# Moving a down projection out of a TensorE-bound feed-forward stage and into the out-projection sums of a scan stage

## The reference, cut to what matters

```python
xn = _layernorm(x, axis=-1)
x = x + attn(xn, ...) + ffn(xn, ...)
...
def ffn(x, w_gate, w_up, w_down):          # H, I = 512, 1408
    gate = fp4_linear(x, w_gate)           # fp4_linear quantises both operands in blocks of 16
    y = fp4_linear(x, w_up)
    h = silu(gate) * y
    return fp4_linear(h, w_down)           # quantises h, 1408 -> 512: the down projection
...
def attn(x, W_in, conv_w, ...):            # a selective scan, D_INNER 1024, 16 states
    x_branch, z = split(x @ W_in)
    xc = silu(conv(x_branch) + conv_b)     # 4 taps
    B, C, dt = split(xc @ W_x)
    h = h * exp(dt * A) + dt * xc * B      # for every token, per channel and state
    y = (sum over states of h * C + xc * D) * silu(z)
    return y @ W_out                       # 1024 -> 512: the out-projection
```

## Time and profile before

| | |
|---|---|
| time, median of 3 runs | 5827.97 us (5827.87 to 5835.2) |
| profiled execution, its own time | 5827.07 us |
| its span | 5824.2 us |
| weight stage | 0 to 178 us |
| feed-forward stage | 178 to about 1820 us |
| scan stage | about 1820 to 5824 us |
| busy: PE, DVE, ACT, POOL | 4979.6, 5035.1, 2768.5, 3627.0 us |
| granted TensorE clock, mean | 0.964 of 2.4 GHz |

### The profile page before, as it was taken

How to read it: one execution, slowest core, us unless ns; L and a number is a source line. 1 busy time by engine, 2 the same in 40 slices (tenths; PEclk the granted TensorE clock), 3 DMA queues, 4 the chain that set the end, 5 groups by cost and what they waited for, 6 DMA issues and landing times.

```text
span 5824.2 us, 78018 instructions
## 1 busy us (share of the span) xinstructions
PE 4979.6 (85%) x21764; PEld 3145.6 (54%) x21764; DVE 5035.1 (86%) x6343; ACT 2768.5 (48%) x4579; POOL 3627.0 (62%) x2810
## 2 busy tenths in 40 slices
PE   1799999999998688888888888888888888888867
PEld 1688888888885344444444444444444444444444
DVE  7666766666662699999999999999999999999998
ACT  1111111111111665666666666666666665666653
POOL 4333333333331687878778788787877878878785
PEclk9999999999999899999999999999999999999968
DMA  2111111111112122222222222222122222222111
GB/s 74 33 42 41 43 40 43 41 41 43 40 42 80 63 77 71 73 73 67 74 71 76 71 65 79 68 76 72 66 74 71 75 71 66 75 71 75 61 56 49
DMA packets 211700, 362.55 MB, mean 62 GB/s; under 512 B 26208, under 2 KB 58976, under 8 KB 207216
## 3 DMA queue, kind: packets, MB, share of 16 engines
q1 hardware_dynamic: 211312, 358.17, 19.9%
HBM read 287.80 MB, written 70.29 MB: 61 GB/s over the span
## 4 chain that ended last, share of the span: by engine, by line
DVE 32%; issue 14%; PE 12%; ACT 5%; POOL 3%; DVEq 1%; DMA 0%; ACTq 0%; SPq 0%; POOLq 0%
DVE hs L1095 20%; DVE acc L1109 11%; PE ht L1212 4%; PE mm L1201 4%; POOL v L919 3%; ACT decay L1056 2%; PE mm L1161 1%; PE mm L1152 1%; DVEq L794 1%; DVE rtb L1081 1%; PE mm L1169 1%; POOL dt L932 1%; ACT xc L981 0%; ACT L1056 0%; ACT dt L1036 0%
## 5 line engine op out<-in xcount | busy, mean ns | idle before, releaser
L919 POOL TENSOR_TENSOR v<-u,b_rep 128x512 f32<-128x512 f32 x2048 | 2578.4, 1274 | 706.7 <-DVE hs L1095 704.7
L1212 PEld LDWEIGHTS ht<-ident,hs 128*128 128x128 f32 x8192 | 957.2, 146 | 1879.8 <-DVE acc L1109 911.4
L1212 PE MATMUL ht<-ident,hs 128*128 128x128 f32 x8192 | 1361.2, 291 | 628.2 <-DVE acc L1109 577.4
L1056 ACT ACTIVATE decay<-dt,a_neg 128x512 f32<-128x512 f32 x2048 | 1376.5, 685 | 607.8 <-DVE hs L1095 586.3
L1109 DVE SCALAR_TENSOR_TENSOR acc<-ht,c_now,acc 128x512 f32<-128x512 f32 x2048 | 1483.7, 725 | 22.9 <-PE ht L1212 22.7
L1095 DVE TENSOR_TENSOR_SCAN hs<-decay,v 128x512 f32<-128x512 f32 x1024 | 1240.4, 1211 | 136.6 <-POOL v L919 111.7
L1095 DVE TENSOR_TENSOR_SCAN hs<-decay,carry,v 128x512 f32<-128x512 f32 x1024 | 1303.2, 1273 | 11.8 <-ACT decay L1056 6.3
L489 ACT ACTIVATE sg<-gate 128x512 f32<-128x512 f32 (+1 forms) x192 | 108.0, 563 | 1331.7 <-PE up L535 1331.7
L1152 PE MATMUL mm<-x_in,w_in 128*128 128x512 f32 x1024 | 527.6, 622 | 20.9 <-DMA x_in<-xnt_d 18.7
L1201 PE MATMUL mm<-w_out,yt 128*128 128x512 f32 x1024 | 536.5, 624 | 7.7 <-ACT xb L966 7.4
L1169 PE MATMUL mm<-w_in,x_z 128*128 128x512 f32 x1024 | 519.1, 610 | 0.0
(11 more groups left out here) (124 smaller groups left out, 6927.3 us busy)
## 6 DMA issues: line engine op xcount, KB each, us to landing
b_rep<-ssm_d SPq DMA_DIRECT2D x512, 256.0 KB, 3.4
tap_diag<-tap_d SPq DMA_DIRECT2D x128, 256.0 KB, 2.9
rtb<-res_d SPq DMA_DIRECT2D x128, 256.0 KB, 4.2
xt<-in_L_attn_x SPq DMA_DIRECT2D x64, 256.0 KB, 2.8
xnt_d<-xntb SPq DMA_DIRECT2D x64, 256.0 KB, 2.7
rt<-in_L_attn_x SPq DMA_DIRECT2D x64, 256.0 KB, 2.7
res_d<-rt SPq DMA_DIRECT2D x64, 256.0 KB, 2.0
x_in<-xnt_d SPq DMA_DIRECT2D x16, 1024.0 KB, 4.8
```

Of the source, the lines that this page charges most:

```text
L919: nc.gpsimd.tensor_tensor(v[k % 2][:, j, :], u[g][:, j, :], b_rep[k % 4][:, :], ALU.mult).then_inc(v_ready, 1)
L1056: nc.scalar.activation(decay[n % 4][:, :], dt[g][:, j, :], ACT.Exp, scale=a_neg[:, GD * g + j, s:s + 1]).then_inc(decay_ready, 1)
L1212: last = nc.tensor.transpose(ht[n % 2][:, j, :], h[k % 2][:, j, t * P:(t + 1) * P], ident[:, :])
```

## The change: the down projection's place, its operands' way, and the order of the feed-forward stage

- Weight stage: w_down is quantised first instead of last. `wd` is then stored to DRAM (`wd_d`, 5.8 MB, two DMAs issued at block 9) and leaves SBUF.
- Feed-forward stage: the product with `wd`, the add of x and the store of `res_d` are gone. The quantised and turned h (`hqt`, now double-buffered, high and low part) is stored to DRAM as `hq_d`, two DMAs of 704 KB for each tile. The normalisation and quantisation of x run two tiles ahead instead of one. The order on DVE, POOL, ACT and TensorE within a tile is new; the PSUM tile `turn` has four buffers instead of two.
- Scan stage: each `wo` sum now begins with products of the down projection, k blocks 0 to 3 of 11 with g = 0 and 4 to 10 with g = 1 (`DOWN`), three matmuls each into the same PSUM bank, and ends with the four out-projection matmuls. That is 44 more units a chunk. Their operands come from DRAM through rings of four buffers: `hq` (128 KB, in pieces of 512 bytes) and `w_dn` (512 KB) for each unit, `dn` in `SP_AT`. `W_in`'s first half is streamed by blocks (`w_ip`, 256 KB, 8 a chunk), `W_out` by halves (1 MB, 2 a chunk). The limit of units is 8/5 a place, and all tables are new. For g = 0 the add takes x from the input, since there is no earlier `res_d`. ACT loads the table set of Exp and Ln by hand behind each group of Silu.

```diff
--- before.py
+++ after.py
@@ phase_w
-    steps = [(w_gate[r * P:(r + 1) * P, :], H, gu, r * P) for r in range(NI)]
+    steps = [(w_down[r * P:(r + 1) * P, :], I, wd, r * P) for r in range(NH)]
+    steps += [(w_gate[r * P:(r + 1) * P, :], H, gu, r * P) for r in range(NI)]
     steps += [(w_up[r * P:(r + 1) * P, :], H, gu, I + r * P) for r in range(NI)]
-    steps += [(w_down[r * P:(r + 1) * P, :], I, wd, r * P) for r in range(NH)]
...
+            if s == NH + 5:
+                sp.wait_ge(w_lo, last_group[NH - 1] + 1)
+                for half in range(2):
+                    sp.dma_start(wd_d.rearrange("k p s n -> p k s n")[:, :, half, :],
+                                 wd[half][:, :, :].bitcast(F32)).then_inc(wd_stored, 16)
...
@@ phase_a, vector: part(t)
-            after, before, done = t.plus(1), t.plus(-1), t.plus(-3)
-            has_h = t.plus(-2).exists(TILES)
-            if done.exists(TILES):
-                dve.wait_ge(rt_loaded[done.p % 2], done.of_parity() * 16)
-                dve.wait_ge(down_done, done.at(1, 1))
-                nc.vector.tensor_tensor(rt[done.p % 2][:, :], down[done.p % 2][:, :], rt[done.p % 2][:, :],
-                                        ALU.add).then_inc(res_ready, 1)
+            before, after, ahead, two = t.plus(-1), t.plus(1), t.plus(2), t.plus(-2)
+            if before.exists(TILES):
+                multiply(before, 2)
+            if ahead.exists(TILES):
+                statistics(ahead)
...
@@ phase_a, gpsimd: part(t)
-                q_x.normalise(nc.gpsimd, xn[:, :], H, after)
-                q_x.scale_back(nc.gpsimd, xq[:, :], H, after)
+                q_x.normalise(nc.gpsimd, xn[:, :], H, ahead)
             if before.exists(TILES):
                 q_h.scale_back(nc.gpsimd, h[before.p][:, :], I, before)
-
-        over_tiles(pool, part, 1, 1)
+            if ahead.exists(TILES):
+                q_x.scale_back(nc.gpsimd, xq[:, :], H, ahead)
+
+        over_tiles(pool, part, 2, 1)
...
@@ phase_a, tensor: part(t)
-                pe.wait_ge(hq_lo, two.at(NT, NT))
-                split_product(down[two.p % 2][:, :], [
-                    ([hqt[s][:, k, :] for s in range(2)], [wd[s][:, k, :] for s in range(2)])
-                    for k in range(NI)]).then_inc(down_done, 1)
...
@@ phase_b
+    DOWN = (range(0, 4), range(4, NK))
...
-                room = (4 * (place + 1)) // 3 - (4 * place) // 3
+                room = (8 * (place + 1)) // 5 - (8 * place) // 5
...
+        def load_down(o, g, t, i):
+            n, k = down_unit(g, t, i), DOWN[g][i]
+            wait(sp, dn_done, o.at(NT * NK, n - 3))
...
+            sp.dma_start(hq[n % 4][:, :, :].bitcast(F32), rows).then_inc(dn_loaded[n % 4], 16)
+            sp.dma_start(w_dn[n % 4][:, :, :].bitcast(F32), wd_d[k]).then_inc(dn_loaded[n % 4], 16)
...
@@ phase_b, tensor: wo
+                if unit < len(DOWN[g]):
+                    m = down_unit(g, t, unit)
+                    wait(pe, dn_loaded[m % 4], o.at(8 * NK * NT, 32 * (m // 4) + 32))
...
+                    nc.tensor.matmul(bank[:, :], left_hi, right_hi, start=first, stop=False)
+                    nc.tensor.matmul(bank[:, :], left_hi, right_lo, start=False, stop=False)
+                    nc.tensor.matmul(bank[:, :], left_lo, right_hi, start=False, stop=False).then_inc(dn_done, 1)
+                    return
```

How the tables place the down units of one `wo` group and its loads (one slot of `SP_AT` in the diff's words):

```diff
+             6: [("tap", 3), ("dn", -1, 1, 0, 4), ("dn", -1, 1, 0, 5), ("dn", -1, 1, 0, 6), ("dn", -1, 1, 1, 0), ("dn", -1, 1, 1, 1), ("dn", -1, 1, 1, 2)],
```

More of the change, by code:

```diff
@@ L163, in sem @@
         return ctx.enter_context(nc.semaphore(name))
+    wd = [sb(f"wd{s}", [P, NI, H], F32R) for s in range(2)]
     raw = [sb(f"w_raw{p}", [P, I]) for p in range(3)]
@@ L356, in part @@
         def part(t):
[L357 removed]
+            ahead, normal, two = t.plus(4), t.plus(2), t.plus(-2)
             if ahead.exists(TILES):
[L359 to L360 removed]
+                if normal.exists(TILES):
+                    sp.wait_ge(ln_vec, normal.at(4, 4))
                 sp.dma_start(xt[ahead.p % 2][:, :], rows(x, ahead)).then_inc(x_loaded[ahead.p % 2], 16)
[L362 to L364 removed]
@@ L376, in _ @@
-        over_tiles(sp, part, 2, 3)
+            if normal.exists(TILES):
+                sp.wait_ge(xnt_copied, normal.at(1, 1))
+                c = normal.p * P
+                dest = (xnt[normal.q, :, :, c:c + P] if isinstance(normal.q, int) else
+                        xnt[bass.ds(normal.q, 1), :, :, c:c + P].rearrange("o p k t -> (o p) k t"))
+                sp.dma_start(dest, xntb[:, :, :]).then_inc(xnt_stored, 16)
+            if two.exists(TILES):
+                sp.wait_ge(hq_lo, two.at(NT, NT))
+                for s in range(2):
+                    tile = (hq_d[two.q, two.p, :, s, :, :] if isinstance(two.q, int) else
+                            hq_d[bass.ds(two.q, 1), two.p, :, s, :, :].rearrange("o p k t -> (o p) k t"))
+                    sp.dma_start(tile, hqt[two.p % 2][s][:, :, :].bitcast(F32)).then_inc(hq_stored[two.p % 2], 16)
@@ L454, in part @@
             if t.exists(TILES):
-                multiply(t, 2)
-            if after.exists(TILES):
-                low_x(t)
-        over_tiles(dve, part, 1, 3)
+                multiply(t, 1)
+            if ahead.exists(TILES):
+                q_x.round(nc.vector, H, ahead)
+            if two.exists(TILES):
+                for g in range(NT):
+                    low_h(t, g)
+        over_tiles(dve, part, 2, 2)
     @block.gpsimd
@@ L672, in sem @@
         return ctx.enter_context(nc.semaphore(name))
-    w_in, w_out = sb("w_in", [P, KH, 2 * DI]), sb("w_out", [P, ND, D])
+    NK = wd_d.shape[0]
+    DOWN = (range(0, 4), range(4, NK))
+    w_z, w_out = sb("w_z", [P, KH, DI]), sb("w_out", [P, GD, D])
+    w_ip = [sb(f"w_ip{p}", [P, KH, P]) for p in range(2)]
+    w_dn = [sb(f"w_dn{p}", [P, 2, D], F32R) for p in range(4)]
+    hq = [sb(f"hq{p}", [P, 2, P], F32R) for p in range(4)]
     w_x_raw = sb("w_x_raw", [P, ND, NR])
@@ L734, in phase_b @@
     for i, part_ in enumerate(MM):
-        for unit in range(UNITS[part_[1]]):
+        for unit in range(units(part_[1:])):
             while room == 0 or place < part_[0]:
                 place += 1
-                room = (4 * (place + 1)) // 3 - (4 * place) // 3
+                room = (8 * (place + 1)) // 5 - (8 * place) // 5
             units_at[place].append((i, unit))
@@ L788, in whose @@
             return c.plus(-1) if g == 1 else c
+        if what == "late_store":
+            return c.plus(-1)
         return c
@@ L866, in move @@
                     load_taps(o, i)
+            elif what == "w_ip":
+                i, = args
+                o = c.plus(1 if i >= 2 else 2)
+                if o.exists(NC):
+                    load_ip(o, i)
+            elif what == "w_out":
+                g, = args
+                o = c.plus(-g)
+                if o.exists(NC):
+                    wait(sp, wo_done, o.at(8, 4 * g))
+                    sp.dma_start(w_out[:, :, :], w_out_rows[:, GD * g:GD * g + GD, :]).then_inc(w_out_loaded, 16)
+            elif what == "dn":
+                owner, g, t, i = args
+                o = c.plus(owner)
+                if o.exists(NC):
+                    load_down(o, g, t, i)
             elif what == "x_in":
@@ L1063, in part @@
                     extra(c, *what)
+                if any(what[0].startswith("silu") for what in ACT_AT.get(n, ())):
+                    nc.scalar.preload_act_table_set(EXP_LN)
         over_chunks(act, part)
@@ L1146, in products @@
                         break
-            bank, first, last = mm[n % 2], unit == 0, unit == UNITS[what] - 1
+            bank, first, last = mm[n % 2], unit == 0, unit == units(task[1:]) - 1
             if what == "ip":
@@ L1151, in products @@
                     wait(pe, x_in_loaded, o.at(16, 16))
-                made, done = nc.tensor.matmul(bank[:, :], w_in[:, k, i * P:(i + 1) * P], x_in[:, k, :],
+                    wait(pe, w_ip_loaded[i % 2], o.at(64, 16 * (i // 2) + 16))
+                made, done = nc.tensor.matmul(bank[:, :], w_ip[i % 2][:, k, :], x_in[:, k, :],
                                               start=first, stop=last), ip_done
```

305 lines of the change are left out of this document (153 added, 152 removed), and 43 rows, old and new, of tables (ACT_AT, MM, POOL_AT).

## The result

The changed kernel took 5869.81 us (median of 5 runs, 5859.48 to 5878.09), beside 5827.87 us for the kernel before (median of 5, 5823.22 to 5835.2). The ratio is 1.0075, interval [1.0063, 1.0087]. The forecast was 5680, in a range from 5450 to 5800: wrong in its sign and outside its range. The profiled execution of the changed kernel has a span of 5868.0 us and took 5869.81.

The account below looks back on a forecast made before the run. It took TensorE to bound the feed-forward stage and VectorE the scan stage. From the 5824.2 us span, -284 + 90 + 28 - 10 + 29 gave 5677, with 2.9 us added 5680; range 5450 to 5800.

Parts of the forecast that it names:

- Feed-forward, both engines: Feed-forward tile: TensorE needs 17.4 us, DVE with two holds 20.7 instead of 25.14, so -284 us over 64 tiles.
- the two holds: Feed-forward tile: DVE operations between SBUF tiles wait for POOL's work on h, 2.1 and 1.3 us a tile.
- (a): Feed-forward tile: DVE's first rounding step of x waits 2.1 us while POOL scales h back.
- (b): Feed-forward tile: DVE's small tensor_scalar of the x scales waits 1.3 us while POOL normalises h.
- Scan stage, TensorE's sum: Scan stage: with the added matmuls TensorE has 219 us a chunk, under DVE's 231 to 240, so alone it costs nothing.
- Scan stage, the loads: Scan stage, g = 1 groups: late down-unit operands cost 1.4 us for each of 64 groups, +90 us, bounds 0 and 400.
- The lateness: Scan stage, g = 1 groups: unit 4's operands come 1.2 us late, units 5 and 6 add 0.5 each, 2.3 us.
- the hidden part: Scan stage: about 1.2 us of each group's lateness is hidden before the add at step 20 that waits for it.
- Rival 3: Scan stage: the load stream moves at half of 399 GB/s, 6.3 us a group, 6030 us in all; chance 0.12.
- Edge of the loop body: Scan stage: PE restarts at half clock with more work a place, 4 us for each of 7 edges, +28 us.
- Both ends: Start of the scan stage -10 us; end behind the last scan +29 us, with units loaded at 1.64 us each.
- Weight stage: Weight stage: storing wd_d and a narrower last block change nothing, taken as zero, from -9 to +15 us.

Follow-up runs that it names:

- e4: The changed kernel with low_h moved ahead of the rounding of x on VectorE in the feed-forward stage: 5771.48 us, ratio 0.9903.
- e6: The kernel before with only the first of the eleven contraction blocks of its down product in each feed-forward tile: 5508.05 us.
- e1: The changed kernel with the down units' operand loads left out after the first four, all matmuls kept: 5568.16 us.
- e3: The changed kernel with three out-projection units between the fourth and fifth down unit of each g = 1 sum, same loads: 5596.15 us.

## Why the prediction was wrong

**Feed-forward, both engines: right.** The tile was 20.63 us for 20.7, by the two holds at the instructions that it named (in 14 of 64 tiles the second one falls on line 407): (a) 2.44 - 0.42 = 2.0 for 2.1 us, (b) 1.67 - 0.18 = 1.5 for 1.3. e4 moved the first one away and got 1.5 us a tile. The Trainium skill's rule of the lock ("SBUF — State Buffer", section "Who interferes with whom"), which the forecast had weighed, would have both held, and the rows agree. What the forecast did not see is that the old order would have reached 20.40 us with the down product gone (e6).

**Scan stage, TensorE's sum: right.** +0 forecast, +3.0 measured with the work and without the loads (e1), give or take the 20 us of e6.

**Scan stage, the loads: this is the step that failed.** The forecast's +90 us, 1.4 for each of 64 groups, was 272.6 us, 4.26 a group (4135.1 less e1's 3862.5). Of its parts:
- The lateness was nearly right: 2.3 us forecast, 0.66 + 1.90 = 2.56 in the group shown, 3.1 in the mean. It was right by luck, through errors that cancel. From a freed buffer to the landing it is by the medians 1.2 of SP and 5.7, so 6.9 us (5.5 and 6.4 in the group shown), and not 4.5; the 2.9 and 4.8 of the earlier trace rows, between which the forecast chose, come from stretches with a mean of 73 GB/s, not 200. But the units passed more slowly too, the fourth of the group shown 3045.34 - 3041.61 = 3.73 us behind the first, 1.24 each and not 1.1. And where the forecast had 1.2, 0.5 and 0.5 us for the fifth, sixth and seventh unit, TensorE waited 0.66, 1.90 and nothing.
- What failed is the price of that lateness, "1.4 us for each of" the groups: the lateness less "about 1.2 us" that is hidden, as if TensorE were on time again once the load is there. The wait puts TensorE's clock to 0.50 for the 5.3 us of work behind it, and the turned states are part of that work. VectorE shows 3.8 us where 2.56 of wait and some 2.5 of slow work come together, which leaves 1.3 hidden; so the hidden part was about right, and the slow work was missing. The earlier trace rows had the half clock after a wait, and the forecast priced it once, at the loop's edge, and not at the waits that it forecast itself.
- It looked for VectorE's stall at the add that needs the sum. It came before that, at `acc`, whose turned states queue on TensorE behind the unit that waits.

**Rival 3, slower: its threshold was right, its mechanism not.** "The change loses as soon as a group costs" 3.7 us holds: 4.26, and it lost. But the stream did not run at half rate. It moved up to 395 GB/s, and e3 hid nearly all of it with an order of the matmuls.

**Edge of the loop body:** +28 forecast; e1's scans are 3.0 us longer than before in all, again give or take 20. **Both ends:** -8.5 for -10 at the start; +52.9 for +29 at the end. e1 splits that into 20.4 of work and 32.5 of loads: with four buffers and units back to back, each of the last four groups waits for a landing of its own, 5.5 to 6.6 us, and that is not a rate of 1.64 us a unit. Behind these waits the clock was down as well (mean 0.79 from 5794 us on, 1.00 behind the last step of e1). **Weight stage:** +6.6, within -9 to +15.

**The range** had its upper end at 5800 because the chance of 0.12 was for one mechanism, a slow stream. It should have carried the chance that a wait costs more than its own length.
